# Linear attention inside a Trainium2 decoder kernel: two halves of 256 tokens with a state between them, in place of one causal 512x512 product

## What is computed

```python
qkv = jax.nn.silu(hidden_states @ qkv_w.T)
...
def step(kv, blk):
    cq, ck, cv = blk
    scores = jnp.einsum('bhnd,bhmd->bhnm', cq, ck) * diag_decay
    intra = jnp.einsum('bhnm,bhmd->bhnd', scores, cv)
    inter = jnp.einsum('bhnd,bhde->bhne', cq * q_decay, kv)
    kv_next = kv * block_decay + jnp.einsum('bhnd,bhne->bhde', ck * k_decay, cv)
    return (kv_next, intra + inter)
...
xf = xf * jax.lax.rsqrt(jnp.mean(xf * xf, axis=-1, keepdims=True) + EPS)
gate = jax.nn.sigmoid(hidden_states @ gate_w.T)
return gate * normed @ out_w.T
```

## Time and profile before

| | us |
|---|---|
| three runs | 1871.03, 1873.34, 1873.51 (median 1873.34) |
| span of the profiled execution | 1870.5 (its first to its last instruction; its own time isn't given apart) |
| TensorE busy | 1807.6 (97%) |
| VectorE busy | 1443.7 (77%) |
| ScalarE busy | 940.1 (50%) |
| POOL busy | 627.6 (34%) |

### The profile page before, as it was taken

The page is one execution under the profiler, slowest core; times in us unless marked ns, Lnnn a source line. Parts: engine busy times, 40 slices in busy tenths (PEclk is TensorE's granted clock), DMA queues, the critical chain, the costliest instruction groups (busy, mean ns, idle before and its releaser), DMA issues.

```text
span 1870.5 us, 26340 instructions
## 1 busy us (share of the span) xinstructions
PE 1807.6 (97%) x9325; PEld 872.7 (47%) x9325; DVE 1443.7 (77%) x2029; ACT 940.1 (50%) x1402; POOL 627.6 (34%) x506
## 2 busy tenths in 40 slices
PE   6999999999999999999999999999999999998887
PEld 4444544444444544444444544444444544564433
DVE  7777777778777777778777777778777777669877
ACT  5554544545454545545454545445354544434664
POOL 2352334324342334324342334324342332301423
PEclk9999999999999999999999999999999999999998
DMA  4112223131322223221321213121221213133332
GB/s 174 65 68 91 69 90 90 69 90 46 119 63 90 69 89 91 76 83 46 119 62 57 70 56 90 57 68 46 85 63 57 71 54 91 58 103 122 113 91 90
DMA packets 117792, 149.64 MB, mean 80 GB/s; under 512 B 67232, under 2 KB 83744, under 8 KB 117280
## 3 DMA queue, kind: packets, MB, share of 16 engines
q1 hardware_dynamic: 106208, 135.29, 22.9%
q0 software_dynamic: 2560, 8.39, 1.4%
q10 hardware_dynamic: 8896, 4.28, 0.8%
HBM read 119.63 MB, written 12.58 MB: 71 GB/s over the span
## 4 chain that ended last, share of the span: by engine, by line
PE 77%; DVE 13%; ACT 4%; issue 4%; DMA 1%; POOL 0%; ACTq 0%; DVEq 0%; SPq 0%; POOLq 0%
PE bank L1296 18%; PE bank L1298 17%; PE bank L1297 17%; PE bank L1269 6%; PE bank L1361 4%; PE bank L1363 3%; PE bank L1362 3%; DVE gated_split L1616 3%; PE bank L1338 2%; PE bank L1340 2%; PE bank L1339 2%; DVE acc L1758 2%; PE bank L1425 1%; PE bank L1436 1%; DVE bank L1676 1%
## 5 line engine op out<-in xcount | busy, mean ns | idle before, releaser
L1296 PE MATMUL bank<-x_blocks,w_pair 128*128 128x512 f16 (+1 forms) x1820 | 678.5, 373 | 12.7 <-DVE bank L1664 7.3
L1298 PE MATMUL bank<-x_blocks,w_pair 128*128 128x512 f16 (+1 forms) x1820 | 678.3, 373 | 0.0
L1297 PE MATMUL bank<-x_blocks,w_pair 128*128 128x512 f16 (+1 forms) x1820 | 678.2, 373 | 0.0
L1876 POOL TENSOR_TENSOR sums_pair<-raw_pair 128x512 f32<-128x512 f32 x63 | 87.0, 1380 | 576.5 <-DVE w_pair L1616 414.6
L1296 PEld LDWEIGHTS bank<-x_blocks,w_pair 128*128 128x128 f16 x1820 | 177.9, 98 | 218.2 <-DVE bank L1664 15.0
L1298 PEld LDWEIGHTS bank<-x_blocks,w_pair 128*128 128x128 f16 x1820 | 178.0, 98 | 202.8
L1297 PEld LDWEIGHTS bank<-x_blocks,w_pair 128*128 128x128 f16 x1820 | 178.1, 98 | 191.0
L1758 DVE TENSOR_TENSOR acc<-acc,bank 128x512 f32<-128x512 f32 x320 | 207.8, 680 | 17.5 <-PE bank L1363 17.5
L1537 ACT ACTIVATE scores_split<-bank 128x512 f16<-128x512 f32 (+1 forms) x192 | 100.6, 526 | 180.9 <-DVE bank L1721 160.7
L1616 DVE SCALAR_TENSOR_TENSOR w_pair<-raw_pair,w_pair 128x1024 f16<-128x1024 f32 x126 | 158.0, 1273 | 34.3 <-ACT w_pair L1489 34.1
L1902 POOL TENSOR_TENSOR ssq<-ssq,sig 128x512 f32<-128x512 f32 x64 | 83.4, 1303 | 282.4 <-ACT sig L1543 281.9
(11 more groups left out here) (212 smaller groups left out, 2637.4 us busy)
## 6 DMA issues: line engine op xcount, KB each, us to landing
raw_pair<-w_qk SPq DMA_DIRECT2D x32, 1024.0 KB, 5.0
raw_pair<-w_gate SPq DMA_DIRECT2D x16, 1024.0 KB, 4.9
raw_pair<-w_out SPq DMA_DIRECT2D x16, 1024.0 KB, 4.9
raw_pair<-w_vt SPq DMA_DIRECT2D x15, 1024.0 KB, 4.9
decay_sb<-decay SPq DMA_DIRECT2D x32, 256.0 KB, 5.3
raw_pair<-ctx_in SPq DMA_DIRECT2D x8, 1024.0 KB, 4.8
acc<-x_t SPq DMA_DIRECT2D x4, 1024.0 KB, 11.5
ctx<-raw_pair SPq DMA_DIRECT2D x8, 512.0 KB, 3.4
```

What stands on the lines that cost most here:

```text
L1296: pe.matmul(out, w_hi, x_hi, start=unmet and k == 0, stop=False, skip_group_check=halves or not fresh)
L1297: pe.matmul(out, w_hi, x_lo, start=False, stop=False, skip_group_check=halves or not fresh)
L1298: mm = pe.matmul(out, w_lo, x_hi, start=False, stop=k == QT - 1, skip_group_check=halves or not fresh)
```

## The change

For pairs 0 to 14 the 512 tokens are cut into two halves of 256. Inside a half the attention goes by tiles as before: key tiles 0 and 2 meet 256 queries, tiles 1 and 3 meet 128. Between the halves stands a state of 128x128 a head and batch: the first half's keys, each times exp(-slope x distance to the half's end), times its values. The second half's queries multiply it, and the result, times a rate per query, is added to the output.

The new parts: the first half's keys stay in float32 in a `sig32` buffer, POOL multiplies them by a rate (`k_decay`), ScalarE and VectorE split them, SP transposes them by DMA (`k_turn`); TensorE makes the state of a head (`state`, 12 matmuls of 128 columns), ScalarE and VectorE split it; in `attend` three matmuls of 256 columns go ahead of the rest, VectorE multiplies their result by the rate and adds it to bank 7, and ScalarE's square waits for that. The decay table is loaded at half its width, and the other half of its buffer takes the rates: four loads of 128 KB a pair. v's product order becomes (1, 7, 2, 6, 4, 5, 3), and in two places `gated` goes behind the next `scores`. The buffer `gated32` goes, its uses are moved. Pair 15 is computed as before (`whole`). The diff, cut to what is named here and in the prediction:

```diff
+HALF_GROUPS = ((0, 2), (1, 3))
+H_OFF = {0: 0, 2: HT, 1: 2 * HT, 3: 2 * HT + P}
+N_HALF = 2 * (HT + P)
...
-    "k": {"p1": "e10", "p6": "w1 w2 l", "p3": "c w0"},
+    "k": {"p1": "e10", "p6": "w1 w2 l", "p5": "j0", "p3": "c w0 j1"},
...
-    def silu(self, done, place, sign, dst, dst_free):
+    def silu(self, done, place, sign, dst, dst_free, kept=False):
+
         gi = self.sig_at % 2
...
+                      slot=self.late_slot, hi=self.tick("qkv_hi"), kept=kept)
         self.sig_free[gi] = st["silu"]
+        self.kept = gi, st["silu"]
         return self.tick("qkv_lo")
...
+        decayed = which == "k" and r % 2 == 0
+        lo = self.silu(done, place, sign, (which, r), [self.qk_free, self.g_split] if which == "k" else
+                       [self.qk_free, self.q_read], decayed)
+        if decayed:
+            gi, silu = self.kept
+            self.release(place, silu)
+            self.decay_keys(r // 2, gi, lo)
+        else:
+            self.release(place, lo)
         for b in range(B):
             self.qk_done[(which, r // 2, b)] = lo
+
+    def decay_keys(self, g, gi, lo):
+
+        self.add("k_decay", g=g, gi=gi, lo=lo, rate=self.rate_ready[g])
+        rate = self.rate_free[g] = self.sig_free[gi] = self.tick("k_rate")
+        self.kd[g] = gi, rate
+
+    def turn_keys(self, g):
+
+        gi, rate = self.kd[g]
+        self.add("k_turn", g=g, gi=gi, rate=rate, free=self.s_free, hi=self.tick("kd_hi"), before=self.q_read)
+        lo = self.sig_free[gi] = self.tick("kd_lo")
+        self.steps[-1]["lo"] = lo
+        self.s_free = self.k_turned[g] = self.tick(f"k_turned{g}", 16)
+
+    def state(self, g):
+
+        i, bank, free = self.main_ring.take()
+        self.add("state", g=g, bank=bank, free=free, turned=self.k_turned[g], v=[t for b in range(B) for t in self.v_done[b][g]],
+                 mm=self.tick("state_mm"), hi=self.tick("st_hi"))
+        self.st_done[g] = self.tick("st_lo")
+        self.main_ring.give(i, self.st_done[g])
 
     def kv_out(self, b, r):
 
...
+    def attend(self, n, unit, whole=False):
...
+        if not whole:
+            j, st["bank2"], st["free2"] = self.main_ring.take()
+            st["state"], st["rate"] = self.st_done[h % GH], self.rate_ready[h % GH]
+            st["inter_mm"], st["inter"], st["joined"] = self.tick("inter_mm"), self.tick("inter"), self.tick("joined")
+            self.main_ring.give(j, st["inter"])
+            self.rate_free[h % GH] = st["inter"]
+            self.q_read = st["mm"]
         self.s_free = st["mm"]
         self.v_hl_free[b] = st["mm"]
...
-            free = [self.g_split, self.g_summed]
-        else:
-            free = [self.scores_mm[1 if unit < 3 else 3]]
         self.add("gated", h=h, b=b, bank=bank, sq=self.attended["sq"], gate=self.gate_done[h % GH], unit=unit,
-                 blocked=blocked, free=free if blocked else [])
+                 blocked=blocked, free=[self.scores_mm[1 if unit < 2 else 3]] if blocked else [])
...
+    def load_decay(self, h, whole=False):
+
         slot = h % 2
-        self.add("decay", h=h, free=self.decay_free[slot])
+        self.add("decay", h=h, free=[self.decay_free[slot]] + ([self.rate_free[slot]] if whole else []), width=S if whole else HT)
         self.decay_ready[slot] = self.tick(f"decay_in{slot}", 16)
...
+    def load_rates(self, n, what):
+
+        for g in range(GH):
+            self.add("rate", h=n * GH + g, what=what, free=self.rate_free[g])
+            self.rate_ready[g] = self.tick(f"rate_in{g}", 16)
...
         product_pair(plan, "gate", n, {
-            "p1": [part(0), part(1)] + [part(2), wo_sum],
-            "p7": [attend(0), gated(0), score(1)],
-            "p6": units(0) + [attend(1), gated(1), score(2)],
+            "p1": [state(0), part(0), part(1)] + [part(2), wo_sum],
+            "p7": [attend(0), score(1), gated(0)],
+            "p6": units(0) + [attend(1), gated(1), score(2), state(1)],
             "p5": [wo(0)],
-            "p4": sums(S3) + [gate(0)] + split_sum(S3) + [wo(1), attend(2), gated(2), score(3)],
+            "p4": sums(S3) + [gate(0)] + split_sum(S3) + [wo(1), attend(2), score(3), gated(2)],
             "p3": [wo(2), gate(1)] + units(2),
         })
...
+        plan.load_rates(n, "k")
         product_pair(plan, "k", n, {
             "p1": stages(4) + stages(5) + ([stash] if stashing else []),
             "p7": stages(6),
             "p2": stages(7),
             "p6": [part(0)] + stages(8) + [part(1)] + stages(9),
-            "p5": stages(10) + [part(2)],
+            "p5": stages(10) + [part(2)] + [turn(0)],
             "p4": stages(11),
             "p3": [part(0)],
         })
+        plan.load_rates(n, "q")
         product_pair(plan, "v", n, {
-            "p1": stages(12) + [part(1)],
+            "p1": stages(12) + [turn(1), part(1)],
             "p7": stages(13) + [part(2)],
             "p2": stages(14),
             "p6": stages(15) + [lambda: plan.scores(n, UNITS[0])],
-        })
+        }, (1, 7, 2, 6, 4, 5, 3))
...
+        self.k_t = self.s_kt[:, 3 * S:7 * S].rearrange("p (h n b i d) -> p h n b i d", h=GH, n=2, b=B, i=2)
...
-        self.g32[0] = self.gated32[:, :]
-        self.v_units = [self.s_hl[:, :, :].rearrange("p n s -> p (n s)")[:, 0:2 * S]]
+        self.g32 = {unit: k_flat[:, unit * D:(unit + 1) * D].bitcast(F32) for unit in UNITS}
+        self.v_units = [self.s_kt[:, 0:2 * S]]
...
+        elif kind == "k_turn":
+            sp.wait_ge(sem["kd_lo"], st["lo"][1])
+            until(sp, sem, st["before"])
+            sp.dma_start(c.k_t[:, st["g"]].rearrange("p n b i d -> p (n b i) d"), c.kd,
+                         transpose=True).then_inc(sem[f"k_turned{st['g']}"], 16)
...
-            for group, part in zip(SCORE_GROUPS, st["parts"]):
+            for group, part in zip(c.scores_of(st)[0], st["parts"]):
                 until(pe, sem, part["free"])
                 bank, width = c.banks[part["bank"]], 0
                 for j in group:
-                    n, cols, keys = S - P * j, slice(j * P, S), slice(j * P, (j + 1) * P)
-                    mm = three(pe, bank[:, width:width + n], [((k[:, 0, keys], k[:, 1, keys]), (q[:, 0, cols], q[:, 1, cols]))])
+                    n = width_of(j, st["whole"])
+                    cols, keys = slice(j * P, j * P + n), slice(j * P, (j + 1) * P)
+                    mm = three(pe, bank[:, width:width + n], [((k[:, 0, keys], k[:, 1, keys]), (q[:, 0, cols], q[:, 1, cols]))],
+                               st["whole"] or j == group[0])
                     width += n
...
+            whole, (_, s_hl, off) = st["whole"], c.scores_of(st)
+            if not whole:
+                until(pe, sem, st["free2"])
+                pe.wait_ge(sem["st_lo"], st["state"][1])
+                state = [c.k_t[:, st["h"] % GH, n, b, 0] for n in range(2)]
+                q = c.units["q"][:, st["h"] % GH, :, b, HT:S]
+                three(pe, c.banks[st["bank2"]][:, 0:HT], [(state, (q[:, 0], q[:, 1]))]).then_inc(sem["inter_mm"])
             for j in range(ST):
-                at = slice(S_OFF[j], S_OFF[j] + S - P * j)
-                vh, vl = (c.v_hl[:, j // 2, n, b, j % 2, st["h"] % GH] for n in range(2))
-                sh, sl = c.s_hl[:, 0, at], c.s_hl[:, 1, at]
-                pe.matmul(bank[:, j * P:S], vh, sh, start=j == 0, stop=False)
-                pe.matmul(bank[:, j * P:S], vh, sl, start=False, stop=False)
-                mm = pe.matmul(bank[:, j * P:S], vl, sh, start=False, stop=j == ST - 1)
+                n = width_of(j, whole)
+                at, to = slice(off[j], off[j] + n), slice(j * P, j * P + n)
+                first, last = (j == 0, j == ST - 1) if whole else (j % 2 == 0, j % 2 == 1)
+                vh, vl = (c.v_hl[:, j // 2, n_, b, j % 2, st["h"] % GH] for n_ in range(2))
+                sh, sl = s_hl[:, 0, at], s_hl[:, 1, at]
+                pe.matmul(bank[:, to], vh, sh, start=first, stop=False)
+                pe.matmul(bank[:, to], vh, sl, start=False, stop=False)
+                mm = pe.matmul(bank[:, to], vl, sh, start=False, stop=last)
             mm.then_inc(sem["attend_mm"])
+        elif kind == "state":
+            g, bank = st["g"], c.banks[st["bank"]]
+            until(pe, sem, st["free"])
+            until(pe, sem, st["turned"])
+            for token in st["v"]:
+                until(pe, sem, token)
+            for b in range(B):
+                mm = three(pe, bank[:, b * HD:(b + 1) * HD],
+                           [([c.k_t[:, g, n, b, i] for n in range(2)], [c.v_hl[:, 0, n, b, i, g] for n in range(2)])
+                            for i in range(2)])
+            mm.then_inc(sem["state_mm"])
...
+            src = c.sig32[st["gi"]][:, :] if st["kept"] else src
...
+            if not st["whole"]:
+                act.wait_ge(sem["joined"], st["joined"][1])
             act.activation(c.sig32[st["gi"]][:, :], bank[:, :], ACT.Square).then_inc(sem["sq"])
+        elif kind == "k_turn":
```

(33 more changed lines are left out.)

110 lines of the change are left out of this document (70 added, 40 removed).

## The result

After the change the kernel takes 1958.03 us (median of four runs, 1957.65 to 1958.86) against 1872.31 for the kernel before: ratio 1.0458, 95% interval 1.0444 to 1.0473. The forecast was 1901.5 us and its range ended at 1936. The direction was right, the size was not: 85.7 us lost where 28.3 were expected. The profiled execution has a span of 1957.0 us against 1870.5.

A forecast was written before the change was run, and what follows sets the result against it. TensorE, paying for columns, was taken as the bound. Per pair 4.75 us of waits lost against 2.59 saved, +28.3 us in all, gave 1899 against the 1870.5 span, so 1901.5 us as median; range 1862 to 1936.

The forecast's parts named there:

- Columns: TensorE's matmuls: 1536 fewer columns a unit at 0.4216 ns each, saving 2.59 us a pair.
- wait 1: Stage 10 of the out product starts late behind k_decay and POOL's sums: +1.8 us a pair, ends 0 and 3.0.
- wait 2: Stages 14 and 15: turn(0) and turn(1) lengthen VectorE's chain beyond the slack in v: +0.6 us, ends 0 and 1.3.
- wait 3: Product 3 of v waits for c22, now directly between products 5 and 3: +1.7 us, ends 0.9 and 2.4.
- wait 4: state(0), ahead of gate's product 7, waits for head 0's last transpose: +0.65 us, ends 0 and 2.3.
- The clock: TensorE's clock in the kernel before, read as at the upper level, 2.4 GHz, in every slice but the last.
- attend(3)'s cover: Two products and scores, 6.1 us, hide join, square, gated, next scores; thin, and if gone 0.3 to 1 us a unit.
- rival of the dear narrow matmul: Runs of 12 narrow matmuls: weight loads not hidden, up to 32 us on top, half taken: 1917; 7 in 100.
- VectorE rival: VectorE bounds the attention stretch, gate's p7 to q's p1: 0.5 us x 60 units on top, 1931; 11 in 100.
- Faster: VectorE and POOL catch up, only c22's 0.94 us remains: 25.6 us gained, 1848; 15 in 100.

The follow-up runs named there:

- e1: The changed kernel with head 0's k_decay put behind the value pair's sums in POOL's queue: 1927.98 us, ratio 1.0289.
- e5: e1 with head 1's key product also behind the sums that follow it, turn(0) earlier and turn(1) later: 1899.92 us, ratio 1.0146.
- e3: The changed kernel without POOL's product of keys and rates and without the key rate loads: 1893.84 us, ratio 1.0107.
- e11: e6 with VectorE's rate product and join cut from 256 columns to 16: 1883.95 us, ratio 1.0060.
- e2: The changed kernel with v's products in the old order 5, 4, 3: 1959.17 us, ratio 1.0456.
- e10: e8 with the last two gate sigmoids of ScalarE moved from behind stage 1 to behind the last unit's gated product: 1880.29 us, ratio 1.0037.
- e6: e5 with v's old order, state(0) behind gate's product 7, queries-times-state behind the half's matmuls, weight parts 1 and 2 behind product 2: 1884.95 us, ratio 1.0069.
- e7: e6 with stage 0 of the out product (the seed) ahead of the split of sum S2: 1886.83 us, ratio 1.0075.
- e8: e6 with seed and third sum earlier, queries-times-state first again except unit 0, first pair's constants later: 1890.27 us, ratio 1.0092.
- e12: The kernel before, with POOL making the value pair's first sum seven times in pairs 1 to 14: 1925.37 us, ratio 1.0291.

## Why the prediction was wrong

Against the profiled spans the forecast was 1899 and 1957.0 was measured, so 58 us are missing. A start-to-start gap is 0.16 us longer than the wait that the profile lists for it, so 0.16 per wait is added.

*Columns:* right. Over a pair, the starts' gaps beyond 0.4216 ns a column add up to 9.4 us after and 1.5 before. The 7.8 between, less the 2.59 saved, are the 5.2 us by which an ordinary pair is longer (110.39 against 105.16).

What such a pair loses, in us:

| | forecast | measured |
|---|---|---|
| wait 1 (stage 10, less what stage 11 gives back) | 1.8 | 2.3 |
| wait 2 (stages 14 and 15) | 0.6 | 2.4 |
| wait 3 (c22) | 1.7 | 0.95 |
| wait 4 (transpose) | 0.65 | 0.9 |
| seed before stage 1 | none | 0.8 |
| gaps under 0.15 us, not listed | none | 0.5 |
| sum | 4.75 | 7.8 |

That is 3.1 a pair, 43 us in 14. Four of the pairs are 2.1 longer still (late c22), 8 us. The part ahead of the first attend(0) is 7.5 us longer, and pair 14 came out 0.5 better: 58 us.

*The step that failed: wait 2, "+0.6, ends 0 and 1.3".* It measured 2.4 a pair by its waits, 2.0 by e1 against e5 and 2.3 by e1 against e3, beyond its own upper end, and with 25 us it is the largest part of what is missing. The term counted what `turn(0)` and `turn(1)` put on VectorE, at undisturbed lengths, against the slack. It put two things at nothing: that the product of head 1's keys stands ahead of the sums for the next gate product in POOL's queue, as head 0's does ahead of the value pair's, and that the sums so moved run beside VectorE's splits, which then take 2.08, 1.16 and 2.28 us where e3 has 1.23, 0.68 and 1.23.

*The same in wait 1:* the order of the chain was right to the link, and 2.3 lies within the ends, but POOL's first sum lost 1.0 us beside VectorE's split. The rows with 1.27 and 1.22 were prices without a neighbour, and the change brought neighbours. The trace of before had a hint that the earlier trace rows does not show: over all pairs the third sum (L1879) has a mean of 1412 ns and VectorE's split of 1273.

*The clock.* The earlier trace rows was read as a constant, and it wasn't one. But of its 22 us by the mean clocks only some 5 are time, 3.4 at the start and 2 at c22. The falls behind stage 10 were taken back at stage 14.

*A wait missing altogether: the seed before stage 1,* 7.9 us in 13 waits, so 10 us. The sum named attend(3)'s cover as thin and made a rival of it, but looked for the price at the next unit and not at ScalarE's seed behind it. e11 shows that the join is in that chain.

*The start.* The sum had no term for the first pair. Two waits stand there that the kernel before doesn't have (1.75 us for a value split at 89.9, 2.06 for u3 at 92.5), and the fall of the clock at 90.6.

*Wait 3 (c22)* stood at its least value in ten pairs, though the transpose of value unit 0 took 4.0 us there and not the 3.0 of the sum. Its sum was also added up short: 618.5 plus 4.38 us of operations and six or seven handoffs of 0.07 is 623.3 or more, not 623.0. Why c22 is not later has not been tested; TensorE itself comes later to it by waits 1 and 2. *Wait 4* was 10.5 us in 11 waits against 9.1. The two were added as if independent, and e2 shows that they trade: 26.3 against 25.4.

The rival of the dear narrow matmul is out (0.056 us each in a run of twelve). Of the VectorE rival's extra 30 us in the attention stretch, the seed's 10 are what came. Faster was never near: it needed less than 2.59 us of waits a pair, and only e10 and e6 come close.

Open: why e7's and e10's waits before the stage name no releaser; why four transposes of value unit 0 land late; what the gaps under 0.15 us are; whether a version of the halves can win. Eight placements of the same work (the kernel after and e1, e2, e5 to e8, e10) lie between 1880 and 1959 us, each time with the next wait close behind the one removed.

## What to carry to other kernels

An operation added to a helper engine should be priced by what stands behind it in that engine's queue and by who reads SBUF beside it, not by its own 1.27 us: 38 us of POOL work cost 64 us here, and e5 got 58 back by order alone. On a chain with four tenths of a microsecond of slack, ask of each wait taken away which one stands directly behind it, since two waits on one chain are one bound. The same holds for the slow clock. A fall cost 1.5 to 3 us in e12, where no long wait followed it, and nothing in the kernel after, where the next wait shrank by as much. So the mean clock is no price in time: compare whole pairs with a fall and without one.

## What was not expected of the hardware

The granted clock fell to 1.2 GHz at 8 of 14 waits of stage 10 of 2.6 us, at 2 of 14 waits of 1.9 us in e8, at 8 of 8 of 4.2 us and more in e12, and at none of 6 of 0.6, for 3.4 us and up to 6.8. At 401 us that was a microsecond after TensorE had resumed; in e12 at 843.51 us it was down at the first matmul already (0.40 to the next start). Page rows in 40 slices do not show it (all nines); the mean clock of the span and windows of a few microseconds do.
